# Layer norms by rows, the softmax subtraction on VectorE, and a new order of the work in each turn

## What is computed

```
z, f, o = tanh(conv(x)), sigmoid(conv(x)), sigmoid(conv(x))   # window of 2 tokens
c_t = f_t * c_(t-1) + (1 - f_t) * z_t ;  h = o * c
n = layernorm(h)                                              # over the 128 features
q, k, v = n @ W_qkv + b_qkv ; gate = sigmoid(n @ W_gate + b_gate)
scores[o] = q . (k shifted by offset o, scaled) + bias        # offsets 0..32, 48, 64, 96, 128, 192, 256
h = h + (softmax(scores) @ v_shifted * gain * gate) @ W_out + b_out
n2 = layernorm(h)
y = gelu(n2 @ W1 + b1) @ W2 + b2        # the same weights for all 64 experts
h = h + y * (router's weight of the kept picks, at most 128 tokens to an expert)
```

## Time and profile before

| | |
|---|---|
| median of 3 runs | 496.3 us (495.8 to 497.25) |
| the profiled execution | 499.14 us, its span 497.3 us |
| granted PE clock, mean over the span | 0.991 |
| busy share of the span | PE 95%, DVE 81%, POOL 80%, ACT 61% |
| share of the chain that ended last | PE 79%, DVE 6%, POOL 5% |

### The profile page before, as it was taken

The page is one execution under the profiler, slowest core; times in us unless marked ns, Lnnn a source line. Parts: engine busy times, 40 slices in busy tenths (PEclk is TensorE's granted clock), DMA queues, the critical chain, the costliest instruction groups (busy, mean ns, idle before and its releaser), DMA issues.

```text
span 497.3 us, 12720 instructions
## 1 busy us (share of the span) xinstructions
PE 473.4 (95%) x4698; PEld 298.6 (60%) x4698; DVE 404.3 (81%) x837; ACT 303.0 (61%) x539; POOL 396.5 (80%) x444
## 2 busy tenths in 40 slices
PE   7689799999999999999999999999999999999994
PEld 5334446465665666666566556656655666658673
DVE  3678797888888898888789788888978889878764
ACT  4456566665765756566475657657555665747664
POOL 6299989997987879698878969878796988986511
PEclk9799999999999999999999999999999999999999
DMA  6000539080724417081542707145180633535901
GB/s 246 15 1 1 132 62 190 11 181 2 180 28 115 94 58 150 2 192 16 129 79 57 151 1 181 27 112 97 52 157 1 164 45 94 100 96 97 192 18 31
DMA packets 54222, 44.27 MB, mean 89 GB/s; under 512 B 27248, under 2 KB 41488, under 8 KB 54032
## 3 DMA queue, kind: packets, MB, share of 16 engines
q1 hardware_dynamic: 54160, 43.45, 39.5%
HBM read 24.59 MB, written 18.85 MB: 87 GB/s over the span
## 4 chain that ended last, share of the span: by engine, by line
PE 79%; DVE 6%; POOL 5%; issue 4%; DMA 4%; ACT 2%; SPq 1%; POOLq 0%; DVEq 0%; ACTq 0%
PE bank L367 19%; PE bank L353 8%; PE bank L462 7%; PE bank L485 6%; PE bank L332 6%; PE bank L333 5%; PE bank L430 4%; PE bank L417 3%; PE bank L341 2%; PE bank L346 2%; PE bank L409 2%; PE bank L381 2%; PE bank L437 2%; PE bank L442 2%; PE bank L447 2%
## 5 line engine op out<-in xcount | busy, mean ns | idle before, releaser
L1140 POOL TENSOR_TENSOR prod<-q,k 128x1496 f32<-128x1496 f32 x48 | 144.0, 3014 | 13.3 <-ACT q L630 13.3
L850 DVE SCALAR_TENSOR_TENSOR prod<-bank,par,k 128x1496 f32<-128x1496 f32 x80 | 139.5, 1768 | 7.5 <-ACT q L630 7.5
L1182 POOL TENSOR_TENSOR acc<-acc,tmp 128x310 f32<-128x310 f32 (+4 forms) x80 | 64.8, 810 | 38.4 <-DVE tmp L907 24.1
L367 PE MATMUL bank<-prod,ew 128*32 128x374 f32 x1024 | 90.3, 481 | 0.8 <-DVE mixin L817 0.8
L1125 POOL TENSOR_TENSOR fprod<-q,k 128x374 f32<-128x374 f32 (+6 forms) x112 | 80.2, 746 | 0.0
L654 ACT ACTIVATE scT<-bank 128x374 f32<-128x374 f32 x48 | 23.2, 484 | 64.8 <-PE bank L367 64.8
L353 PE MATMUL bank<-xn,par 128*128 128x374 f32 x128 | 53.7, 506 | 2.9 <-DVE xn L839 2.9
L485 PEld LDWEIGHTS bank<-par,hid 128*128 128x128 f32 x384 | 47.6, 191 | 9.9 <-issue 6.8
L367 PEld LDWEIGHTS bank<-prod,ew 128*32 128x32 f32 x1024 | 28.9, 110 | 37.6 <-issue 34.7
L485 PE MATMUL bank<-par,hid 128*128 128x128 f32 x384 | 50.1, 275 | 0.9 <-ACT hid L713 0.9
L907 DVE TENSOR_TENSOR tmp<-bank,vT 128x310 f32<-128x310 f32 (+4 forms) x80 | 30.3, 380 | 23.9 <-PE bank L409 22.2
(11 more groups left out here) (130 smaller groups left out, 977.4 us busy)
## 6 DMA issues: line engine op xcount, KB each, us to landing
band_scratch<-attn SPq DMA_DIRECT2D x16, 769.5 KB, 6.0
band<-band_scratch SPq DMA_DIRECT2D x64, 192.0 KB, 3.8
v<-v_scratch SPq DMA_DIRECT2D x32, 192.0 KB, 5.0
v_scratch<-vtok SPq DMA_DIRECT2D x16, 192.0 KB, 4.1
xT<-x_dram SPq DMA_DIRECT2D x16, 187.5 KB, 4.2
out_dram<-osb SPq DMA_DIRECT2D x16, 128.0 KB
par<-params_dram SPq DMA_DIRECT2D x1, 1819.5 KB, 7.7
out_dram<-osb SPq DMA_DIRECT2D x16, 59.0 KB
```

The source lines that it names most:

```text
L367: done = mm(home(f"s{c}")[32 * g:32 * g + 32, 0:N], ew[:, c * CW + j, :], src[:, j, :], start=first or only, stop=last or only)
L850: v.scalar_tensor_tensor(bass.AP(prod[c][:, :, :].tensor, part * N, [[CW * N, 128], [PARTS * N, w], [1, N]]), home("q")[:, 0:N].unsqueeze( ...
L1140: g.tensor_tensor(bass.AP(prod[c][:, :, :].tensor, part * N, [[CW * N, 128], [PARTS * N, w], [1, N]]), q[q_.s][:, :].unsqueeze(1).broadcas ...
L1182: g.tensor_tensor(acc[:, o:N], acc[:, o:N], tmp[i % 2][:, o:N], ALU.add).then_inc(acc_added[i], 1)
```

## The change

Both layer norms are made by rows. PE turns `h` (three transposes, `turn_h`); DVE takes mean and variance of each token (`bn_stats`, `bn_aggr`, three tiles each) and computes `shift = -mean * rstd`; Ln and Exp on ACT run over 128x3; ACT writes `x * rstd + shift` in three instructions (`norm1_rows`), PE turns the result back (`turn_x`), and ACT copies it to `xn` (`norm1_back`). `center`, `variance`, the two squares and DVE's two multiplications are gone. The copy of `h` for the residual is made by ACT from the turned `h` (`keep_rows`) and POOL adds the output bias to it (`carry`). `out_project` has its operands swapped and writes rows (three matmuls of 128 columns in place of one of 374), so `residual` makes `h2` by rows; `h2` is turned only after its norm (`turn_x2`), and `turn_h2` is gone.

The seven scores of the last chunk (offset 0 and the far ones) get three transposes and a `score_add` of their own, in place of L384 and L867; the far offsets are ordered so that the odd half of that chunk starts at column 96. `score_subtract` is a DVE instruction. `add_b2` works in place in PSUM and waits for all three `down`. The table `HOME` and the order of `turn` are new on PE, DVE, ACT and POOL; SP issues `write_attn` a turn later by its own count.

```diff
-            def center(q_, *before):
+            def turn_h(q_, *before):
...
-                mm(home("hc")[:, 0:N], P("cen4"), h[q_.s][:, :], start=True, stop=True).then_inc(hc_mm, 1)
-            def variance(q_, *before):
...
-                mm(home("var")[:, 0:N], P("avg"), stat[:, :], start=True, stop=True).then_inc(var_mm, 1)
+                for t in range(TT):
+                    done = tr(home("ht")[:, t * 128:(t + 1) * 128], h[q_.s][:, t * 128:(t + 1) * 128], ident)
+                done.then_inc(h_turned, 1)
+            def turn_x(q_, *before):
+                freed(pe, before)
+                pe.wait_ge(xrow_ready, q_.b + 1)
+                for t in range(TT):
+                    done = tr(home("xb")[:, t * 128:(t + 1) * 128], xrow[:, t, :], ident)
+                done.then_inc(x_turned, 1)
...
+                lo = SHORT if c == CH and not first else 0
...
             def out_project(q_, *before):
...
-                mm(home("op")[:, 0:N], P("outw"), ao[:, :], start=True, stop=True).then_inc(out_mm, 1)
+                for t in range(TT):
+                    done = mm(home("op")[:, t * D:(t + 1) * D], ao[:, t * 128:(t + 1) * 128], P("outw"), start=True, stop=True)
+                done.then_inc(out_mm, 1)
...
+            def norm1_rows(q_):
+                act.wait_ge(shift_ready, q_.b + 1)
+                after(act, x_turned, q_.b)
+                for t in range(TT):
+                    done = A(xrow[:, t, :], home("ht")[:, t * 128:(t + 1) * 128], ACT.Identity,
+                             bias=shift[:, t:t + 1], scale=rstd[:, t:t + 1])
+                done.then_inc(xrow_ready, 1)
...
-            def norm1(q_):
...
-                v.tensor_tensor(xn[q_.s][:, :], home("hc")[:, 0:N], stat[:, :], ALU.mult).then_inc(xn_ready, 1)
+            def stats1(q_):
+                dve.wait_ge(h_turned, q_.b + 1)
+                for t in range(TT):
+                    done = v.bn_stats(part[:, t, :], home("ht")[:, t * 128:(t + 1) * 128])
+                done.then_inc(part_ready, 1)
+                dve.wait_ge(part_ready, q_.b + 1)
+                after(dve, rstd_ready, 2 * q_.b)
+                for t in range(TT):
+                    done = v.bn_aggr(stat[:, t, :], part[:, t, :])
+                done.then_inc(stat_ready, 1)
+
+            def shift_rows(q_):
...
+                v.scalar_tensor_tensor(shift[:, :], stat[:, :, 0], -1.0, rstd[:, :], ALU.mult, ALU.mult)\
+                    .then_inc(shift_ready, 1)
...
+            def score_subtract(q_):
+                dve.wait_ge(mx_ready, q_.b + 1)
+                v.tensor_tensor(sc[:, :, :], sc[:, :, :], mx[:, :].unsqueeze(2).broadcast_to([128, TT * HEADS, NO]),
+                                ALU.subtract).then_inc(sub_ready, 1)
...
-            def score_subtract(q_):
-                pool.wait_ge(mx_ready, q_.b + 1)
...
             def add_b2(q_):
-                dve.wait_ge(down_mm[0], q_.b + 1)
+                dve.wait_ge(down_mm, TT * (q_.b + 1))
```

More of the change, by code:

```diff
@@ L18 @@
 NFAR = len(FAR)
-OFFS = [LOCAL - j for j in range(DENSE)] + FAR
+FAR_ORDER = [96, 48, 128, 64, 192, 256]
+OFFS = [LOCAL - j for j in range(DENSE)] + FAR_ORDER
 NO = len(OFFS)
@@ L486, in down @@
                               P("down", f * D, (f + 1) * D), start=(f == 0), stop=(f == FC - 1))
[L487 to L494 removed]
+                done.then_inc(down_mm, 1)
             def turn(at):
@@ new lines, in turn @@
+                if a1:
+                    turn_h(a1, ("ht", a2))
+                if a2:
+                    score(a2, 0, 3, ("op", a4), ("pv", a4), ("dn", a6), ("s0", a3), first=True)
+                    score(a2, 0, 2)
+                    score(a2, 0, 1)
+                    score(a2, 0, 0, last=True)
+                    score(a2, 1, 1, ("bc0", a3), ("fw", a3), ("up0", a5), ("up3", a5), ("tb0", a4), ("x2b", a5), ("ts1", a3), ("s1", a3), first=True)
+                    score(a2, 1, 3)
+                    turn_scores(a2, 2, ("s2", a2))
@@ L517, in turn @@
+                if a3:
+                    spread_far(a3, 2, ("q", a2), ("bc4", a4))
+                if a2:
+                    score(a2, 1, 0)
+                    score(a2, 1, 2, last=True)
+                if a3:
+                    spread_far(a3, 3, ("bc1", a3))
                 if a5:
-                    up(a5, 0, ("th", a6), ("k", a1))
+                    down(a5, 2, ("s0", a2), ("op", a4), ("pv", a4), ("dn", a6), head=True)
                 if a2:
-                    turn_scores(a2, 1, ("up1", a5), ("tb2", a4), ("bc4", a4), ("hc2", a5), ("ts1", a3))
@@ L1041, in turn @@
                 if a4:
-                    norm2(a4)
+                    shift2_rows(a4)
                 if a0:
-                    norm1(a0)
+                    recur(a0)
                 if a3:
                     far_value(a3, 3)
+                if a5:
+                    gate_sum(a5)
                 if a2:
-                    softmax_sum(a2)
+                    score_add(a2, 0)
+                    score_add(a2, 1)
                 if a3:
@@ L1230, in turn @@
                 if a1:
-                    score_subtract(a1)
-            pipeline(pool, turn, 5)
+                    local_products(a1, 3)
+                    local_products(a1, 1)
+                    local_products(a1, 2)
+                if a2:
+                    far_sum(a2, 1)
+                if a4:
+                    kept_mask(a4)
+                    kept_weights(a4)
+                if a2:
+                    far_sum(a2, 2)
+                    far_sum(a2, 3)
+                    far_sum(a2, 4)
+                if a0:
+                    far_products(a0, 0, head=True)
+                    far_products(a0, 1)
+                if a2:
+                    far_sum(a2, 5)
+                    carry(a2)
+                if a1:
+                    far_attention(a1)
+            pipeline(pool, turn, 4)
 def _params(i):
```

614 lines of the change are left out of this document (295 added, 319 removed).

## The result

The changed kernel takes 493.98 us (median of 9 runs, 493.14 to 494.92), beside 497.29 us for the kernel before on the same chip (9 runs, 495.8 to 498.92): ratio 0.9929, 95% interval 0.9912 to 0.9947. That is 3.3 us less, where 13 were forecast. The direction was right and the time lies in the range; the size was not. The profiled execution took 493.53 us, its span 491.2.

The account below looks back on a forecast made before the run. DVE was to set a full turn at 27.9 us; fill 73, twelve turns 332, drain 62.6 and tail 16.4 gave a span of 484 us, a median time of 483, range 469 to 499.

Parts of the forecast that it names:

- DVE as the bound: In a full turn DVE's work of 27.3 us passes PE's 26.1 and sets the turn.
- the sum of -2.4: PE's work in a full turn, from matmuls and transposes removed and added: 28.5 - 2.4 = 26.1 us.
- DVE's sum: DVE's work in a full turn: 24.7 - 1.26 + 1.08 + 0.25 + 2.5 = 27.3 us (26.8 to 28.5).
- The port: POOL and DVE can hold each other up; in the layout POOL waits while DVE subtracts, so nothing was charged.
- the rival prices at 2.8 us: DVE's subtraction waits for a POOL product, 1.4 us on average; turn 29.0 at most, time 495; chance 0.07.
- The turn: A full turn: 27.3 us of DVE work plus 0.6 us of waits, 27.9 us.
- the one through `p10_ready`: PE's `spread_far` waits for DVE's products; 26.4 us long with hand-overs, PE may lose about 1 us.
- the slower rival: Waits at `p10_ready` and at `up` behind the gate's tanh don't hide; turn 29.9, time 505 us; chance 0.13.
- The four parts: Span of 484 us: fill 73, twelve turns 332, drain 62.6, tail 16.4; 13 less than 497.3.
- The scale: From span to time: 484, 486 as a profiled execution, 483 as median, which lies 2.8 below 499.14.
- DVE dearer: Norms on DVE cost 1.8 us each with 1 us of waits; turn 29.0, time 495 us; chance 0.12.
- PE bound: Small DVE instructions run at their lower bounds and all waits hide; turn 26.8, time 471 us; chance 0.13.

Follow-up runs that it names:

- the clock held: Changed kernel with 18 dummy matmuls behind the first `turn_h`, then 5 more before sequence 0's second score chunk: 493.04 us (18) and 493.91 us (23).
- the first experiment: Changed kernel with each `bn_stats` of `stats2` made once more into a spare tile, 0.67 us a turn more on DVE: 499.25 us, ratio 1.0007.

## Why the prediction was right in direction and wrong in size

**DVE as the bound: wrong.** This is the step that failed in kind: a turn set by DVE's 27.3 us over PE's 26.1. PE's work is 27.03, so the sum of -2.4 should have been -1.5, and PE, with one gap, sets the turn. The sum took only instructions that vanish or appear. The order changed what the kept ones cost as well. `attend` is the clearest: before,

```profile
271.77 1.20 PE L430 MATMUL bank<-bandT,v 128*32 128x32 f32 x64
272.78 0.82 PE L367 MATMUL bank<-prod,ew 128*32 128x374 f32 x8
273.41 0.64 PE L430 MATMUL bank<-bandT,v 128*32 128x32 f32 x32
273.87 0.48 PE L367 MATMUL bank<-fprod,ew 128*32 128x374 f32 x1
```

its 96 records took 1.01 + 0.46 = 1.47 us from start to start; now they take 0.61 + 1.17 = 1.78 (234.20 to 234.81, and 236.27 to the end at 237.44; with the gap filled, 0.62 + 1.10 = 1.72 from start to start). `out_project` takes 0.82 in place of 0.67, `turn_h` 0.46 in place of 0.32, `spread_far` 0.85 in place of 0.65 (mean of four turns, summed from start to start). The far and last scores take 1.37 us as before, so the 0.16 for their narrower half never came. That is 0.96, and 0.3 came back on `project`, `down` and `positions`; small rests make up the missing 0.9.

The rows show what most of these have in common. A matmul uses 128 columns of the array or 32 (`128*128` and `128*32` in the rows; scores and `attend` are of the second kind). Two records of L362 of 374 columns, ahead of an `attend`, take 0.72 us from start to start (235.55 to 236.27); two of L336, ahead of their own kind, 0.62 (240.01 to 240.63). Over seven full turns of each trace a 374-column matmul of the first kind has 0.314 us to a next one of its kind and 0.407 to one of the second, in both kernels. On the way back, four scores abreast take 0.43 us to the next matmul where they take 0.31 to the next four, and the first 374-column matmul behind them 0.42 where others take 0.31. The order of before goes over from one kind to the other 6 times a turn, the new one 12 times. Three more of each at 0.09, and at 0.1 to 0.2, are 0.6 to 0.9 us: an estimate from these distances, which no run tested by moving such a change of kind alone. The forecast had no term for it.

**DVE's sum: about right.** Forecast 27.3 (26.8 to 28.5) on a base of 24.7 busy; by the same measure it is 26.5, a little under the range, and 26.8 where only the two waits of 0.24 and 0.58 are left out of the turn. Three `bn_stats` 0.70 and three `bn_aggr` 0.23 to 0.31 were as priced, both norms together 2.35 against 2.5, the subtraction 1.13 against 1.08. Two errors went against each other: `softmax_out` grew by 0.7 beside POOL's `carry`, and the kept instructions took some 1.5 less, `rs * gain` for one (L887 before, 0.411 in the earlier trace rows) now 0.163.

**The port: charged nothing, and nothing was lost.** The contention came, at 0.7 us a turn, not on the subtraction but on `softmax_out`. The Trainium skill (SBUF — State Buffer, § Who interferes with whom) says that a DVE instruction with two SBUF inputs and a GpSimd instruction that reads SBUF exclude each other for their whole length. The trace agrees: `softmax_out` started 0.17 us after `carry`, ended 0.7 us late, and POOL's next instruction waited for it in turn. As DVE is not the bound, the turn did not notice. (The block of POOL that the rival prices at 2.8 us is 8.96 / 3 = 2.99 in the earlier trace rows.)

**The turn: near by luck.** 27.9 forecast, 27.61 measured, with another engine as the bound. Of the forecast's two rings, the one through `p10_ready` never showed a wait; the one named in passing in the slower rival, `up` behind the gate's tanh and its table load, is the 0.58 us. PE idle was to be 1.5 to 2 us, mostly before L410 or L377; neither shows any in a full turn.

**The four parts.** In time the fill is the term that missed most: 78.9 against 73. The first products came at 27.45 against 26 (with the clock held, at 25.98, so this part is the lower clock); then the early turns took 18.6, 22.3 and 25.1 us against 18, 20 and 21. POOL shows it:

```profile
27.45 4.94 POOL L1178 TENSOR_TENSOR fprod<-q,k 128x374 f32<-128x374 f32 x7 [19.42 <-ACT q L631]
...
46.09 5.83 POOL L1178 TENSOR_TENSOR fprod<-q,k 128x374 f32<-128x374 f32 x7 [4.73 <-ACT k L637]
...
68.39 6.05 POOL L1178 TENSOR_TENSOR fprod<-q,k 128x374 f32<-128x374 f32 x7 [1.13 <-ACT k L637]
```

Of the turn that starts at 46.09 only 1.7 us are waits and 20.6 are work, with far attention and far sums already in it; I had counted the products and too little else. These turns were called POOL's and yet never added up from POOL's rows, which the trace of before had. Twelve turns 327.9 against 332 and drain 65.3 against 62.6 were near; the drain's three turns took 26.2, 23.8 and 15.2 us against 26.0, 23.1 and 13.5 (before 22.9, 16.6, 14.3). That is where two thirds of the steady gain went back, and there more work on DVE did cost time, as the first experiment shows; what sets the drain was not taken further. Tail 19.1 against 16.4: the store takes from 487.33, when `finish` ends, to 491.2, 3.9 us where I had 2.2, and `add_b2` starts 13.8 us after the output projection. In span: +5.9, -4.1, +2.7, +2.7 = +7.2.

**The scale.** The other 3.8 us are no mechanism. The profiled execution of before was 1.85 us above the median of its nine runs, that of after 0.45 below; and the median of three (496.3) was 1 us below that of nine. The forecast subtracted 2.8 us as if it belonged to the kernel. A forecast of a change of 3 us can't be made from one execution and three runs with a spread of this size.

**The chances.** "Faster" at 0.76 was borne out. The rival "DVE dearer", with 495 us, came nearest in time and was wrong in its mechanism. The rival "PE bound", at 0.13, named the engine that the runs show, but expected it at a turn of 26.8 us and 471 us.

## What to carry to other kernels

When the bound of a tuned kernel moves by little, look for gaps in the engine with the most work before counting the second engine: here a gap of 0.22 us on PE made the turn 0.22 longer, and filling one of 0.58 made it 0.51 shorter, which was worth more than the whole change; where another engine's wait lay just below (0.47 us moved for 0.08, 0.63 us removed for 0.34), less came. When an order is rewritten, count how often PE changes between matmuls of different width. Before calling a gap fillable, see what stands just behind the moved instruction on every queue, the DMA queue included. An added instruction tests for a bound only if it isn't put where the engine is idle. And an early turn of a pipeline is priced from the rows of the engine that sets it, all of its instructions, not the main ones.

## What was not expected of the hardware

- A merged group of records can hide a wait: three `up` at 2.54 us in place of 2.15 were 0.39 us of waiting, shown as busy.
- 96 matmuls of 32 columns took 1.47 us from start to start in one order and 1.72 in another, with the same operands. A 374-column matmul took 0.314 us to the next of its kind and 0.407 to one that uses 32 columns of the array; the new order has 12 changes of kind in a turn, that of before 6.
- A pause of PE in the fill moved the granted clock of later stretches: 0.50 from 20 to 30 us in the changed kernel, 0.50 from 37.2 to 40.6 with dummies in the first pause, 0.50 from 40 to 45 with another order, and with 23 dummies 1.00 up to 55.1 us and 0.50 from there to 58.5.
- DVE's `softmax_out` took 0.98 us alone and 1.68 when it began 0.17 us after POOL's 1.01 us `carry`.
